# Layer 0 experts of a four-layer model: picks as moving operand, rows fetched ten experts ahead, sums loaded in four parts

## The reference, cut to what matters

```
E, K, H, I, CAP = 32, 6, 256, 128, 96
h = x.reshape(-1, Hd)                       # 1024 tokens, normalised
scores = sqrt(softplus(h @ gate_w.T))
topk_idx = top_k(scores + bias, K)          # 6 experts a token
topk_w = scores[topk_idx] / sum * 1.5
pos = running number of the token within its expert;  valid = pos < CAP
xb[eid, pos] = h                            # 96 rows for each expert
inter = silu(xb @ w_gate.T) * (xb @ w_up.T)
yb = inter @ w_down.T
routed = sum over the token's 6 experts of yb[eid, pos] * w_slot
shared = clip(silu(h @ sg.T) * (h @ su.T), -10, 10) @ sd.T
return routed + shared
```

## Time and profile before

| what | us |
|---|---|
| median of 3 runs (lowest, highest) | 1340.66 (1339.51, 1341.48) |
| the profiled execution's own time | 1330.74 |
| its span, first to last instruction | 1329.0 |
| TensorE matmuls busy | 1090.4 (82%) |
| VectorE busy | 809.9 (61%) |
| ScalarE busy | 612.5 (46%) |
| GpSimd busy | 534.2 (40%) |

### The profile page before, as it was taken

One profiled execution on the slowest core, in us unless ns is written; L12 is line 12 of the kernel. 1 busy time (PEld: TensorE's weight loads), 2 busy tenths in 40 slices (PEclk: granted clock), 3 DMA queues, 4 the chain that ended last, 5 costly groups with the idle time before them and its releaser, 6 DMA issues.

```text
span 1329.0 us, 18665 instructions
## 1 busy us (share of the span) xinstructions
PE 1090.4 (82%) x6235; PEld 881.6 (66%) x6235; DVE 809.9 (61%) x2031; ACT 612.5 (46%) x1709; POOL 534.2 (40%) x566
## 2 busy tenths in 40 slices
PE   5969987188966992579999999999996587795894
PEld 2559654054754882578988889988985466475783
DVE  3672222265545888767887877878774656455343
ACT  1520443101211223468788887878784141362252
POOL 1600577445432553334454454444531054131453
PEclk7855999688986996679999999999997778897997
DMA  8200588500000002001101011010000250003394
GB/s 354 97 5 1 140 208 191 150 1 0 0 13 13 12 1 115 32 1 49 48 1 49 1 48 49 1 49 1 17 2 0 82 137 1 0 1 143 98 339 147
DMA packets 43726, 86.39 MB, mean 65 GB/s; under 512 B 9200, under 2 KB 27664, under 8 KB 41968
## 3 DMA queue, kind: packets, MB, share of 16 engines
q1 hardware_dynamic: 36256, 72.34, 16.0%
q0 software_dynamic: 7376, 12.87, 4.3%
HBM read 67.11 MB, written 18.08 MB: 64 GB/s over the span
## 4 chain that ended last, share of the span: by engine, by line
PE 50%; DVE 18%; issue 15%; POOL 9%; ACT 4%; DMA 4%; SPq 0%; DVEq 0%; POOLq 0%; ACTq 0%
PE bank L186 28%; PE bank L195 7%; PE bank L2268 3%; DVE a_qn L2421 3%; PE bank L1186 2%; PE bank L2257 2%; POOL a_qk_rstd L234 2%; POOL sum L1057 1%; DVE a_catw L2056 1%; DMA sum<-f_ys,f_index 1%; POOL a_q_rstd L234 1%; POOL f_got L1049 1%; PE bank L436 1%; POOL f_xs L2017 1%; DVE stats L220 1%
## 5 line engine op out<-in xcount | busy, mean ns | idle before, releaser
L2719 POOL TENSOR_TENSOR a_p<-a_p,a_tot 128x128 f32<-128x128 f32 x64 | 52.0, 832 | 211.3 <-DVE a_tot L2392 211.3
L982 ACT ACTIVATE swi_gated<-bank 128x128 f32<-128x128 f32 (+1 forms) x87 | 24.0, 276 | 143.8 <-PE bank L186 143.8
L2443 DVE TENSOR_REDUCE a_top<-bank 128x2 f32<-128x512 f32 (+1 forms) x96 | 57.7, 602 | 35.5 <-PE bank L2268 21.8
L186 PE MATMUL bank<-a_proj_high,a_catq 128*128 128x256 f32 x256 | 69.2, 304 | 12.0 <-DVE a_catq L2062 9.0
L2660 ACT ACTIVATE a_cat<-bank,a_ismooth 128x256 bf16<-128x256 f32 x128 | 50.3, 481 | 51.9 <-PE bank L2303 51.9
L2421 DVE TENSOR_SCALAR a_qn<-bank,a_qk_minus,a_qk_rstd 128x128 f32<-128x128 f32 x192 | 64.0, 403 | 5.9 <-issue 3.2
L186 PE MATMUL bank<-a_proj_low,a_catq 128*128 128x256 f32 x256 | 67.1, 296 | 0.0
L2588 ACT ACTIVATE a_qn<-bank,a_q_shift,a_q_rstd 128x128 f32<-128x128 f32 x128 | 48.3, 460 | 40.6 <-POOL a_q_shift L237 40.6
L2268 PE MATMUL bank<-a_kt,a_qt 128*128 128x256 f32 x256 | 65.2, 400 | 0.0
L195 PE MATMUL bank<-const,rows 128*128 128x128 f32 x96 | 19.8, 392 | 53.4 <-ACT rows L267 50.8
L186 PE MATMUL bank<-cols,a_vs 128*128 128x256 f32 x256 | 63.4, 392 | 0.0
(11 more groups left out here) (440 smaller groups left out, 3540.5 us busy)
## 6 DMA issues: line engine op xcount, KB each, us to landing
expert<-in_experts SPq DMA_DIRECT2D x42, 384.0 KB, 3.9
f_expert<-in_experts SPq DMA_DIRECT2D x23, 384.0 KB, 6.4
a_raw_w<-in_groups SPq DMA_DIRECT2D x8, 1024.0 KB, 6.0
a_raw_proj<-in_groups SPq DMA_DIRECT2D x8, 512.0 KB, 3.9
f_xs<-l_zero SPq DMA_DIRECT2D x1, 3999.0 KB, 20.6
l_expert<-in_experts SPq DMA_DIRECT2D x10, 384.0 KB, 7.2
f_got<-f_xs SPq DMA_DIRECT2D x6, 516.0 KB, 8.4
l_weights<-in_l SPq DMA_DIRECT2D x1, 2784.0 KB, 21.3
```

The lines of the kernel that those rows point to most:

```text
L186: ins = pe.matmul(out, lhs, rhs, start=start and n == 0, stop=stop and n == len(pairs) - 1, skip_group_check=shared)
L2443: v.tensor_reduce(top[:, cs], src, AX.X, ALU.max, negate=True).then_inc(*s["top_ready"].one())
L2719: g_.tensor_tensor(cross_probs(m, ti), cross_probs(m, ti), over(m.tot[n % 2][:, first:first + HPG], SC), ALU.mult).then_inc(*s["cross_weig ...
```

## The change

- The product with the picks is turned round. `facts` (128x2) is the stationary operand, and the 3072 picks of a tile are the moving one, in six matmuls of 512 columns, into banks 1, 2, 3, 5, 6 and 7. The result is two rows of 3072 numbers, on 2 partitions.
- VectorE copies three of the banks to `row`, ScalarE three, after the last tile. SyncE then spreads `row` over 96 partitions into `table` with two SBUF-to-SBUF DMAs. The index waits for both. TensorE starts the shared expert only after the six copies, whose banks it needs. The table's two parts lie apart, for the DMAs.
- `counts`, both `picks` tiles, `row` and now 16 buffers for gathered rows (`DEEP_GOT`) share one block of memory, `pool`. The scatters follow the gathers ten experts behind (`AHEAD`) instead of five.
- `counts` is written in four instructions.
- The sums are loaded in four pairs of DMAs of 256 KB, two tiles each, and VectorE alone adds them, two tiles at a time; GpSimd adds none.
- Landing semaphores are shared by name with those of the last layer.

```
--- before.py
+++ after.py
@@ -689,24 +689,30 @@
 
 TILES0 = NT
 DEEP = 4
-DEEP_GOT = 6
+
+DEEP_GOT = 16
+AHEAD = 10
+
+PICK_BANKS = (1, 2, 3, 5, 6, 7)
+PAIRS = NT // 2
 
 
 LAYER0F = dict(pe="gate_made place_made picked swi_opened swi_flipped shared_made got_flipped experts_closed",
-               v="gate_copied gate_plus mask_ready weights_ready place_ready pick_ready swi_inner indexed got_copied "
+               v="gate_copied gate_plus mask_ready weights_ready place_ready pick_ready row_copied_v swi_inner indexed got_copied "
                  "x_added",
-               a="gate_exp gate_log swi_gated swi_turned shared_copied y_copied",
-               g="zeroed facts_set counted x_pooled")
+               a="gate_exp gate_log row_copied_a swi_gated swi_turned shared_copied y_copied",
+               g="zeroed facts_set counted")
 
 
 def layer0_ffn(k):
     with ExitStack() as scope:
         m = Box()
         s = k.stage(NORM, VALUES, KEYS, LAYER0F)
-        for name, kind in (("h_rows_out", Landing), ("sum0_out", Landing), ("sum1_out", Landing),
-                           ("sums_in", Landing), ("f0_added0", Landing), ("f0_added1", Landing),
-                           *((f"f0_got{n}_in", Landing) for n in range(DEEP_GOT))):
-            s[name] = k.sema(name, kind)
+        for n, name in enumerate(("h_rows_out", "sum0_out", "sum1_out", "table_in",
+                                  *(f"sums{n}_in" for n in range(PAIRS)))):
+            s[name] = k.landing(f"block{n}_moved")
+        for n, name in enumerate(("f0_added0", "f0_added1", *(f"f0_got{n}_in" for n in range(DEEP_GOT)))):
+            s[name] = k.landing(f"rows{n}_moved")
         sb = lambda name, shape, dt=F32: k.sb(name, shape, dt, scope)
         n_rows = TOK + SINK
         m.n_rows = n_rows
@@ -731,16 +737,19 @@
         m.total = sb("f0_total", [P, NT])
         m.place = sb("f0_place", [P, NT, E0], BF16)
         m.facts = sb("f0_facts", [P, NT, 2], BF16)
-        m.counts = sb("f0_counts", [P, CAP, E0], BF16)
-        m.picks = [sb(f"f0_pick{n}", [P, CAP, E0], BF16) for n in range(2)]
+        size = CAP * E0 // 2
+        m.pool = sb("f0_pick", [P, 3 * size])
+        grid = lambda n: m.pool[:, n * size:(n + 1) * size].bitcast(BF16)
+        m.counts, m.picks = grid(2).rearrange("p (c e) -> p c e", e=E0), [grid(0), grid(1)]
+        m.row = m.pool[0:2, 0:CAP * E0]
         m.gated = [sb(f"swi_gated{n}", [P, I]) for n in range(3)]
         m.inner = [sb(f"swi_inner{n}", [P, I]) for n in range(3)]
         m.turned = [sb(f"swi_turned{n}", [P, I]) for n in range(3)]
-        m.table = sb("f0_table", [CAP, E0, 2])
+        m.table = sb("f0_table", [CAP, 2, E0])
         m.number = sb("f0_number", [CAP, E0])
         m.empty = sb("f0_empty", [CAP, E0])
         m.index = sb("f0_index", [CAP, E0], U32)
-        m.got = [sb(f"f0_got{n}", [CAP, D + E0]) for n in range(DEEP_GOT)]
+        m.got = [m.pool[0:CAP, n * (D + E0):(n + 1) * (D + E0)] for n in range(DEEP_GOT)]
         m.cols = [sb(f"f0_cols{n}", [P, DC, CAP]) for n in range(3)]
         m.ys = [sb(f"f0_ys{n}", [CAP, D]) for n in range(DEEP)]
         layer0_ffn_sync(k, m, s)
@@ -748,7 +757,7 @@
         layer0_ffn_vector(k, m, s)
         layer0_ffn_scalar(k, m, s)
         layer0_ffn_pool(k, m, s)
-        k.x_ready = [[s["x_added"].at(i // 2 + 1) if i % 2 else s["x_pooled"].at(i // 2 + 1)] for i in range(NT)]
+        k.x_ready = [[s["x_added"].at(i // 2 + 1)] for i in range(NT)]
 
 
 def tiled(dram):
@@ -770,6 +779,11 @@
     on.wait_ge(*s["weights_ready"].at(1))
     q.dma_start(m.h_rows[0:TOK, D:D + E0].rearrange("(t p) e -> p t e", p=P), m.weight[:]).then_inc(
         *s["h_rows_out"].one())
+    on.wait_ge(*s["row_copied_v"].at(3))
+    on.wait_ge(*s["row_copied_a"].at(3))
+    for f in range(2):
+        q.dma_start(m.table[:, f, :], m.row[f:f + 1, :].rearrange("f (c e) -> f c e", e=E0)).then_inc(
+            *s["table_in"].one())
     on.wait_ge(*s["shared_made"].at(NT))
     fetch_expert(k, len(k.experts))
     on.wait_ge(*s["shared_copied"].at(NT // 2))
@@ -781,8 +795,10 @@
             fetch_expert(k, e)
     for n in range(2):
         on.wait_ge(*s[f"f0_added{n}"].at(E0 // 2))
-    q.dma_start(k.x[:], tiled(m.sums[0])).then_inc(*s["sums_in"].one())
-    q.dma_start(m.shared[:], tiled(m.sums[1])).then_inc(*s["sums_in"].one())
+    for n in range(PAIRS):
+        for sums, to in zip(m.sums, (k.x, m.shared)):
+            q.dma_start(to[:, 2 * n:2 * n + 2, :], tiled(sums)[:, 2 * n:2 * n + 2, :]).then_inc(
+                *s[f"sums{n}_in"].one())
 
 
 def swiglu_open(k, s, bank, rows, cols, slot):
@@ -813,14 +829,16 @@
     on.wait_ge(*k.kq_scaled.at(H1 // 2))
     for r in range(NT):
         on.wait_ge(*s["pick_ready"].at(r + 1))
-        for x in range(E0):
-            ins = pe.matmul(k.bank[6][0:CAP, 2 * x:2 * x + 2], m.picks[r % 2][:, :, x], m.facts[:, r, :],
-                            start=r == 0 and x == 0, stop=r == NT - 1, skip_group_check=True)
+        for n, bank in enumerate(PICK_BANKS):
+            ins = pe.matmul(k.bank[bank][0:2, :], m.facts[:, r, :], m.picks[r % 2][:, n * BANK:(n + 1) * BANK],
+                            start=r == 0, stop=r == NT - 1)
         ins.then_inc(*s["picked"].one())
     slot, came = expert_slot(k, 0)
     _, down = expert_weights(slot)
     on.wait_ge(*came)
     on.wait_ge(*s["place_ready"].at(1))
+    on.wait_ge(*s["row_copied_v"].at(3))
+    on.wait_ge(*s["row_copied_a"].at(3))
     for r in range(NT + 2):
         if r < NT:
             on.wait_ge(*s["swi_turned"].at(r - 2))
@@ -935,14 +953,16 @@
     on.wait_ge(*s["counted"].at(1))
     for i in range(NT):
         on.wait_ge(*s["picked"].at(i - 1))
-        v.tensor_tensor(m.picks[i % 2][:], under(m.place[:, i, :], CAP), m.counts[:], ALU.is_equal).then_inc(
+        v.tensor_tensor(m.picks[i % 2].rearrange("p (c e) -> p c e", e=E0), under(m.place[:, i, :], CAP), m.counts, ALU.is_equal).then_inc(
             *s["pick_ready"].one())
 
     on.wait_ge(*s["picked"].at(NT))
     table = m.table
-    v.tensor_copy(table[:].rearrange("p e f -> p (e f)"), k.bank[6][0:CAP, 0:E0 * 2]).then_inc(*step.one())
-    on.wait_ge(*step.now())
-    v.tensor_tensor(m.number[:], table[:, :, 0], table[:, :, 1], ALU.add).then_inc(*step.one())
+    for n in range(3):
+        v.tensor_copy(m.row[:, n * BANK:(n + 1) * BANK], k.bank[PICK_BANKS[n]][0:2, :]).then_inc(
+            *s["row_copied_v"].one())
+    on.wait_ge(*s["table_in"].at(2))
+    v.tensor_tensor(m.number[:], table[:, 0, :], table[:, 1, :], ALU.add).then_inc(*step.one())
     on.wait_ge(*step.now())
     v.tensor_scalar(m.empty[:], m.number[:], 0.0, c["slot1"][0:CAP, :], ALU.is_equal, ALU.mult).then_inc(*step.one())
     on.wait_ge(*step.now())
@@ -970,9 +990,10 @@
             on.wait_ge(*s["swi_flipped"].at(n - 2))
             v.scalar_tensor_tensor(m.inner[n % 3][0:CAP, :], k.bank[n % 3][0:CAP, I:2 * I], m.got[x % DEEP_GOT][:, D + x:D + x + 1],
                                    m.gated[n % 3][0:CAP, :], ALU.mult, ALU.mult).then_inc(*s["swi_inner"].one())
-    on.wait_ge(*s["sums_in"].at(2))
-    for i in range(1, NT, 2):
-        v.tensor_tensor(k.x[:, i, :], k.x[:, i, :], m.shared[:, i, :], ALU.add).then_inc(*s["x_added"].one())
+    for n in range(PAIRS):
+        on.wait_ge(*s[f"sums{n}_in"].at(2))
+        pair = slice(2 * n, 2 * n + 2)
+        v.tensor_tensor(k.x[:, pair, :], k.x[:, pair, :], m.shared[:, pair, :], ALU.add).then_inc(*s["x_added"].one())
 
 
 def swiglu_gate_scalar(k, s, m, n, rows):
@@ -996,6 +1017,10 @@
     a.activation(t["log1p"][:], t["one_plus"][:], ACT.Ln).then_inc(*s["gate_log"].one())
     layer1_fold_scalar(k, s, m.fold, range(2, len(KEY_BANKS)))
     layer1_keys_scalar(k, s)
+    on.wait_ge(*s["picked"].at(NT))
+    for n in range(3, len(PICK_BANKS)):
+        a.activation(m.row[:, n * BANK:(n + 1) * BANK], k.bank[PICK_BANKS[n]][0:2, :], ACT.Copy).then_inc(
+            *s["row_copied_a"].one())
     for r in range(NT + 2):
         if r < NT:
             swiglu_gate_scalar(k, s, m, r, P)
@@ -1039,26 +1064,26 @@
     g.tensor_copy(m.facts[:, :, 0], k.c["tokpart"].broadcast_to([P, NT]))
     g.tensor_scalar(m.facts[:, :, 1], k.c["iota_e"][:, 0:NT], float(P), 0.0, ALU.mult, ALU.add).then_inc(
         *s["facts_set"].one())
-    g.tensor_scalar(m.counts[:], over(k.c["iota_c"], E0), 1.0, 0.0, ALU.add, ALU.add).then_inc(*s["counted"].one())
+    for n in range(4):
+        cs = slice(n * CAP // 4, (n + 1) * CAP // 4)
+        ins = g.tensor_scalar(m.counts[:, cs, :], over(k.c["iota_c"][:, cs], E0), 1.0, 0.0, ALU.add, ALU.add)
+    ins.then_inc(*s["counted"].one())
     on.wait_ge(*s["indexed"].at(1))
     on.wait_ge(*s["h_rows_out"].at(3))
-    for r in range(E0 + 5):
+    for r in range(E0 + AHEAD):
         if r < E0:
             on.wait_ge(*s["got_flipped"].at(r - DEEP_GOT + 1))
             on.wait_ge(*s["swi_inner"].at(NT + r - DEEP_GOT + 1 if r >= DEEP_GOT else 0))
```

(9 more changed lines are left out.)

99 lines of the change are left out of this document (62 added, 37 removed).

## The result

The changed kernel took 1326.18 us (1325.46 to 1328.42, 4 runs) against 1341.07 of the kernel before beside it (1339.51 to 1345.76, 4 runs): ratio 0.9886, 95% interval 0.9859 to 0.9913. That is faster by 14.9 us. 1310.0 was predicted, 30.7 us less, with 1302 to 1322 as the range: the sign was right, the size half of what was said.

The account below looks back on a forecast made before the run. TensorE's number of instructions was taken to bound the picks, GpSimd the experts, then a serial end. Gains of 24.1 + 4.1 + 2.2 = 30.4 us off 1340.66 gave 1310; own range 1306 to 1314, with rivals 1302 to 1322.

Parts of the forecast that it names:

- up to the first scatter: Layer 0, picks to first scatter: shared expert starts at 107.5 instead of 131.62, first scatter at 128.7; 24.1 us earlier.
- ten ahead, to the last scatter: Routed experts: with gathers ten ahead, 21 instead of 26 stand between scatters; last scatter at 217.3, 4.1 us gained.
- sums, to the first statistics: End of layer 0: loading the sums in four parts makes 11.9 us into 9.7, 2.2 us less (0.8 to 3.0).
- all that follows: Everything behind the next layer's first statistics: no gain or loss was counted there.
- Picks, row, table, index: Ahead of the shared expert and gathers: picks end at 105.2, shared expert starts at 107.5, first gather at 111.3.
- rival 1: TensorE's picks: low clock throughout, 2.56 us a tile, all that follows 5.1 us later, 1315 us; chance 0.30.
- rival 4: Transfer of the row into the table: much slower than any row shows, 1324 us at a 20 us landing; chance 0.04.
- rival 5: Scatters bound from their start by landings: gain gone from 7.6 us a landing, 1354 us at 8.5; chance 0.03.
- I take 21.2 unchanged, between -1.9 and +1.1: Shared expert's start to first scatter: still 21.2 us, as index waits and a full clock give about as much back.
- Counts in quarters: GpSimd's counts ahead of the picks, in four instructions: effect taken as 0, between -2.4 and +0.5 us.
- The tail, "I take 2.4": Last ten scatters, with no gather between: 2.4 us each, against 2.68 before, as weight fetches crowd only the first half.
- Carried over: Whole kernel: the 9.9 us between profiled execution (1330.74) and median (1340.66) stay, so the 30.4 us come off the median.

Follow-up runs that it names:

- stalling: Kind of chip (or set of runs) on which the kernel before, unchanged, took 1341 to 1344 us; four of six sets, the result's among them.
- third set's trace of before: The kernel before, unchanged, profiled on a stalling chip: 1344.18 us (8 runs); the profiled execution took 1338.92.
- quiet: Kind of chip (or set of runs) on which the kernel before, unchanged, took 1331 us; two sets, and the profile used for the prediction is like these.
- first set's of the changed kernel: The changed kernel, unchanged, profiled anew on a quiet chip: 1309.78 us (4 runs), ratio 0.9843 of the kernel before.
- second profile of the kernel before: The kernel before, unchanged, profiled anew on a quiet chip: 1332.49 us (10 runs) beside 1331.54; the profiled execution took 1336.89.
- the row held: Changed kernel with its seventh to eleventh gathers held until TensorE made the shared expert's last tile: 1307.56 us on a quiet chip, 1324.04 on a stalling one.
- three sums: Changed kernel with scatters dealt to three sum buffers instead of two, the third's zeroing, load and addition left out: 1314.61 us.

## Why the prediction was wrong

By its own steps, gains in us against the kernel before on the same kind of chip (stalling: third set's trace of before against the result's; quiet: the profile used for the prediction against the first set's of the changed kernel):

| step | predicted | stalling | quiet |
| --- | --- | --- | --- |
| up to the first scatter | 24.1 | 17.0 | 22.0 |
| ten ahead, to the last scatter | 4.1 | 2.2 | 0.0 |
| sums, to the first statistics | 2.2 | 1.4 | 2.1 |
| all that follows | 0 | -8.0 | -3.3 |
| sum (profiled span) | 30.4 | 12.6 | 20.8 |
| medians | 30.7 (1340.66 - 1310.0) | 14.9 | 21.8 |

The lower rows are no better than two profiles of one kernel agree. Held against the second profile of the kernel before, on the first set's own chip, the quiet column reads 22.0, 3.7, 1.6 and -0.3, in sum 26.9. And the third set's trace of before is that kernel's shortest execution of eight, 5.3 us under their median, which makes the stalling column's gains small.

- **Picks, row, table, index: right.** Picks end 105.04 (105.2) with the clock full from 95.2, after two tiles at 2.56 us each; row copies 0.63 us each (0.69), table landing 2.7 us from the first issue (2.7). The low clock through the picks (rival 1) didn't come. The slow table (rival 4) and the slower scatters (rival 5, longest landing 5.9 us in the quiet profile) didn't either.
- **"I take 21.2 unchanged, between -1.9 and +1.1" is the step that failed.** From the shared expert to the first scatter the result took 29.35 us, 24.9 in the quiet set. Shown: 7 us are lost with a row of gathers longer than six (gone with five ahead, and with the row held), by late signals of TensorE and the low clock behind them. On quiet chips 3.7 us go to the low clock after the two waits (21.4 from first gather to first scatter with it, 17.7 without), where the prediction counted the waits as bare time; that the waits let the clock fall is likely by the count above, not shown. The swap of the wait behind the index for a full clock was right: TensorE began the third tile 3.9 us after the first (111.09 against 107.20), before 3.8, and where neither stall nor low clock came the whole stretch took 21.2 us. The eleven gathers were priced (13.6 us, measured 13.5) but only on GpSimd's own account, as if beside them all else ran free.
- **Counts in quarters: about right.** The picks began at 89.77 (89.82 before) in the result's run and at 88.84 in the quiet one: 0 to 1 us. In two other stalling profiles they began at 92.05 and 92.08, 2.2 us later and over the bound of 0.5; the reason is open.
- **The tail, "I take 2.4", was 2.65 (2.71 quiet).** The mechanism named, a wait for the landing two back, was the right one, which three sums show; the reason to expect less, fetches out of the way in its second half, bore nothing: they are issued until 219.4, two thirds into the tail, and the scatters behind are no faster. Over ten scatters that is 2.5 to 3 us of the miss. The 21 experts before it took 64.9 us (64.6 predicted).
- **"Carried over" from a profile of 1330.74 to a median of 1340.66 failed, and all that follows was put at nothing.** The 9.9 us are stalls in layer 3's row of 16, and no constant: 10.5 us before, 11.9 after (37.8 - 25.9). The rest of what layer 3 lost, 3 us ahead of its row and 3 in it, goes with the clock at 0.5 from 1187 to 1225 in one piece (before: 1207 to 1218 and 1221 to 1235). The one long piece of 37.5 us is in 11 of the 12 profiles of kernels with the change or parts of it and two sums, in none of the 4 with three sums, and in 1 of the 3 of the kernel before. So it isn't the change's alone, but may be likelier with it; that is open.
- Whether the new semaphore names have a part in layer 3 wasn't tried. That its stalls were there before the change, nearly as long, speaks against it.
